# A mixture-of-experts kernel on one Trainium2 core: expert weights loaded tile by tile at a register's address, and held stationary in the up projections

## What is computed

```python
logits = xf @ gate_w.T                      # 8 experts
wts, idx = jax.lax.top_k(logits, 1)         # softmax over one: weight 1
h = silu(xf @ w1[e].T) * (xf @ w3[e].T)     # 128 -> 512, e the token's expert
y = h @ w2[e].T                             # 512 -> 128
y = y + gelu(xf @ sw1.T) @ sw2.T            # shared expert
```

## Time and profile before

| | us |
|---|---|
| median of three runs | 335.92 (335.11 to 340.64) |
| span of the profiled execution | 334.8 |
| PE busy | 234.4 (70%) |
| DVE busy | 170.4 (51%) |
| ACT busy | 106.4 (32%) |
| POOL busy | 102.7 (31%) |
| PE stage of the experts (first `turn_x` to the last `down`) | 252.2 to 326.9 |

### The profile page before, as it was taken

One profiled execution on the slowest core, in us unless ns is written; L12 is line 12 of the kernel. 1 busy time (PEld: TensorE's weight loads), 2 busy tenths in 40 slices (PEclk: granted clock), 3 DMA queues, 4 the chain that ended last, 5 costly groups with the idle time before them and its releaser, 6 DMA issues. The chain is left out here.

```text
span 334.8 us, 4486 instructions
## 1 busy us (share of the span) xinstructions
PE 234.4 (70%) x1436; PEld 125.6 (38%) x1436; DVE 170.4 (51%) x461; ACT 106.4 (32%) x215; POOL 102.7 (31%) x107
## 2 busy tenths in 40 slices
PE   0071673266197945979746989798946999999990
PEld 0050232112054412434213424356632665665650
DVE  7858999778036601467643772866011233423320
ACT  1000343000055441645432587342500223233230
POOL 9600178500047000640000000000751256556551
PEclk9996587555558585879785999979985899999997
DMA  6400059316163561636230079200222021121100
GB/s 200 148 0 1 0 145 166 130 53 143 72 144 108 141 161 57 133 91 158 71 88 10 5 243 405 109 2 0 81 79 77 25 58 37 43 53 35 35 15 0
DMA packets 21933, 29.46 MB, mean 88 GB/s; under 512 B 3306, under 2 KB 17200, under 8 KB 21912
## 3 DMA queue, kind: packets, MB, share of 16 engines
q1 hardware_dynamic: 20312, 26.81, 28.6%
q0 software_dynamic: 1600, 2.38, 2.7%
HBM read 21.14 MB, written 8.80 MB: 89 GB/s over the span
## 5 line engine op out<-in xcount | busy, mean ns | idle before, releaser
L669 DVE TENSOR_REDUCE smax<-bank 128x2 f32<-128x384 f32 x96 | 50.6, 554 | 59.1 <-PE bank L890 56.9
L476 ACT ACTIVATE p_ring<-bank 128x384 f32<-128x384 f32 x96 | 45.5, 491 | 73.5 <-PE bank L916 72.3
L890 PE MATMUL bank<-stacks 96*128 96x192 bf16 (+1 forms) x256 | 41.8, 316 | 35.2 <-DMA stacks<-split_scratch 33.0
L1067 PE MATMUL bank<-stacks,p_ring 128*128 x76 | 44.0, 666 | 2.1 <-DVE p_ring L792 1.8
L385 POOL TENSOR_TENSOR r<-f_ring,parts 128x384 f32<-128x384 f32 x14 | 12.8, 917 | 91.4 <-ACT f_ring L461 90.9
L890 PEld LDWEIGHTS bank<-stacks 96*128 96x128 bf16 (+1 forms) x256 | 16.5, 120 | 64.7 <-DMA stacks<-split_scratch 35.8
L410 POOL DMA_INDIRECT xs_scratch<-hn,slot_u x12 | 11.8, 982 | 90.4 <-issue 90.4
L916 PE MATMUL bank<-stacks 99*128 99x192 bf16 (+1 forms) x256 | 35.9, 277 | 2.7 <-ACT p_ring L476 2.4
L799 DVE TENSOR_TENSOR stacks<-bank,stacks 128x512 f32<-128x512 f32 x19 | 13.1, 691 | 45.5 <-PE bank L1067 45.5
L540 ACT ACTIVATE stacks<-bank 128x512 f32<-128x512 f32 x19 | 11.3, 597 | 61.8 <-PE bank L1067 61.8
L934 PE MATMUL bank<-p_ring,vaug 128*32 128x384 f32 (+1 forms) x256 | 29.5, 551 | 0.3 <-ACT oT L483 0.3
(11 more groups left out here) (127 smaller groups left out, 301.3 us busy)
## 6 DMA issues: line engine op xcount, KB each, us to landing
split_scratch<-parts SPq DMA_DIRECT2D x16, 288.0 KB, 9.8
stacks<-split_scratch SPq DMA_DIRECT2D x16, 288.0 KB
stacks<-in_w_dram SPq DMA_DIRECT2D x8, 512.0 KB, 7.9
stacks<-split_scratch SPq DMA_DIRECT2D x16, 192.0 KB
stacks<-in_w_dram SPq DMA_DIRECT2D x8, 256.0 KB, 8.1
stacks<-split_scratch SPq DMA_DIRECT2D x16, 96.0 KB
xs_scratch<-empty SPq DMA_DIRECT2D x19, 64.5 KB, 3.2
p_ring<-xs_scratch SPq DMA_DIRECT2D x19, 64.5 KB
```

What stands on the lines that cost most here:

```text
L476: act.activation(p_ring[:, half % 2, g % GH, :, :], bank[2 + g % 2][:, 0:2 * SEQ].rearrange("p (s q) -> p s q", s=2), ACT.Exp).then_inc(ex ...
L669: dve.tensor_reduce(smax[:, p % 2, j, 2 * hd:2 * hd + 2], bank[g % 2][:, 0:2 * SEQ].rearrange("p (s k) -> p s k", s=2), AX.X, ALU.max, neg ...
L890: ins = pe.matmul(bank[g % 2][r0:r0 + rn, SEQ * s:SEQ * (s + 1)], q_st[p % NST][0:SROWS, 2 * hd + s, 128 * j + r0:128 * j + r0 + rn], k_st ...
L1067: pe.matmul(bank[UP_BANKS[m][t % 2]][:, :], xsT[:, t % 2, :], w13_sb[:, bass.ds(e, 1), m, :].rearrange("p a i -> p (a i)"), start=True, st ...
```

## The change

Two things change, both in the expert stage.

1. The eight-expert load ahead of the stage is gone. `load_expert(t)` on SyncE reads `et_i[0, t]` into a register and loads that expert's `w13` and `w2` from DRAM into buffer t mod 3 (NW = 3). The first three are issued as soon as `et_i` is ready; from t = 3 on, `load_expert(t)` waits until `down(t-3)` is done (`y_mm`), and stands in SyncE's stream right behind `load_xs(t)`. All 19 tiles load their weights, also where neighbours have the same expert.
2. The up projections hold the weights stationary and move the 128 tokens: four matmuls of 128 columns in place of one of 512, for w1 and for w3. The result comes out with the 512 on the partitions, as `down` wants it, so `turn_g`, `copy_gT`, their PSUM bank and `gate_sb` are gone, and `gate` writes `gT` itself. PE's order becomes `up(t, 0)`, `turn_x(t+2)`, `up(t, 1)`, `down(t-1)`; the transposed tokens get a third buffer, and `take_x(t+2)` stands ahead of `gate(t)` on VectorE.

```diff
-            for e in range(E):
-                sp.dma_start(w13_sb[:, e, :, :], w13[e, :, :, :]).then_inc(ld_exp, 16)
-                sp.dma_start(w2_sb[:, e, :, :], w2[e, :, :, :]).then_inc(ld_exp, 16)
+            def load_expert(t):
+                if t >= NW:
+                    sp.wait_ge(y_mm, t - NW + 1)
+                e = sp.value_load(et_i[0:1, t:t + 1], min_val=0, max_val=E - 1)
+                sp.dma_start(w13_sb[:, t % NW, :, :], w13[bass.ds(e, 1), :, :, :].rearrange("a p m i -> p (a m) i")).then_inc(w_ld[t % NW], 16)
+                sp.dma_start(w2_sb[:, t % NW, :, :], w2[bass.ds(e, 1), :, :, :].rearrange("a p c d -> p (a c) d")).then_inc(w_ld[t % NW], 16)
...
+            sp.wait_ge(et_done, 1)
+            for t in range(NW):
+                load_expert(t)
             for tc in range(2):
...
             for t in range(NX, SLOT_TILES):
                 load_xs(t)
+                load_expert(t)
...
-            def copy_gT(t):
-                act.wait_ge(g_tr, t + 1)
-                if t >= 2:
-                    act.wait_ge(y_mm, t - 1)
-                act.activation(gT[:, t % 2, :], bank[GT_BANK][:, :], ACT.Copy).then_inc(g_cp, 1)
...
                 if t >= 2:
-                    dve.wait_ge(g_tr, t - 1)
-                dve.tensor_tensor(gate_sb[:, t % 2, :], bank[UP_BANKS[1][t % 2]][:, :], sA[:, t % 2, :], ALU.mult).then_inc(gated, 1)
+                    dve.wait_ge(y_mm, t - 1)
+                dve.tensor_tensor(gT[:, t % 2, :], bank[UP_BANKS[1][t % 2]][:, :], sA[:, t % 2, :], ALU.mult).then_inc(gated, 1)
...
             take_x(0)
+            take_x(1)
             for t in range(SLOT_TILES):
+                if t + 2 < SLOT_TILES:
+                    take_x(t + 2)
                 gate(t)
-                if t + 1 < SLOT_TILES:
-                    take_x(t + 1)
...
-            def up(t, e, m):
+            def up(t, m):
                 pe.wait_ge(x_cp, t + 1)
+                if m == 0:
+                    pe.wait_ge(w_ld[t % NW], 16 * 2 * (t // NW + 1))
...
-                pe.matmul(bank[UP_BANKS[m][t % 2]][:, :], xsT[:, t % 2, :], w13_sb[:, bass.ds(e, 1), m, :].rearrange("p a i -> p (a i)"), start=True, stop=True)\
-                    .then_inc(up_b if m else up_a, 1)
-
-            def turn_g(t):
+                for c in range(IC):
+                    ins = pe.matmul(bank[UP_BANKS[m][t % 2]][:, 128 * c:128 * (c + 1)], w13_sb[:, t % NW, m, 128 * c:128 * (c + 1)],
+                                    xsT[:, t % NXT, :], start=True, stop=True)
+                ins.then_inc(up_b if m else up_a, 1)
...
             for t in range(SLOT_TILES):
-                up(t, e, 0)
-                if t >= 1:
-                    turn_g(t - 1)
-                up(t, e, 1)
-                nxt = expert_of(t + 1) if t + 1 < SLOT_TILES else None
-                if t + 1 < SLOT_TILES:
-                    turn_x(t + 1)
-                if t >= 1:
-                    down(t - 1, prev)
-                e, prev = nxt, e
-            turn_g(SLOT_TILES - 1)
-            down(SLOT_TILES - 1, prev)
+                up(t, 0)
+                if t + 2 < SLOT_TILES:
+                    turn_x(t + 2)
+                up(t, 1)
+                if t >= 1:
+                    down(t - 1)
+            down(SLOT_TILES - 1)
```

More of the change, by code:

```diff
@@ L182, in build_kernel @@
         xs = carve("exp", NX, XW)
-        xsT = carve("exp", 2, D)
+        NXT = 3
+        xsT = carve("exp", NXT, D)
         sA = carve("stack", 2, I)
-        gate_sb = carve("stack", 2, I)
         gT = carve("exp", 2, I)
@@ L194, in build_kernel @@
         ld_x, ld_wn, ld_rows, ld_wp, ld_c, ld_txt, ld_np = [sem(f"ld_{n}") for n in ("x", "wn", "rows", "wp", "c", "txt", "np")]
-        ld_exp = sem("ld_exp")
+        w_ld = [sem(f"w_ld{i}") for i in range(NW)]
         dve_step, pool_step = sem("dve_step"), sem("pool_step")
@@ L227, in build_kernel @@
         xs_ld = [sem(f"xs_ld{i}") for i in range(NX)]
-        x_tr, x_cp, up_a, up_b, silu_done, gated, g_tr, g_cp, y_mm, y_cp = [sem(n) for n in (
-            "x_tr", "x_cp", "up_a", "up_b", "silu_done", "gated", "g_tr", "g_cp", "y_mm", "y_cp")]
+        x_tr, x_cp, up_a, up_b, silu_done, gated, y_mm, y_cp = [sem(n) for n in (
+            "x_tr", "x_cp", "up_a", "up_b", "silu_done", "gated", "y_mm", "y_cp")]
         id_done, base_clear, base_st = sem("id_done"), sem("base_clear"), sem("base_st")
@@ L251, in build_kernel @@
         SH_BANKS, SY_BANKS = (2, 3, 6, 7), (5, 0, 5)
[L252 removed]
+        UP_BANKS, XT_BANK, Y_BANKS, RANK_BANK = ((2, 3), (6, 7)), 4, (5, 0), 4
         def mbank(item):
@@ L789, in take_x @@
                 dve.wait_ge(x_tr, t + 1)
-                if t >= 2:
-                    dve.wait_ge(up_b, t - 1)
-                dve.tensor_copy(xsT[:, t % 2, :], bank[XT_BANK][:, 0:D]).then_inc(x_cp, 1)
+                if t >= NXT:
+                    dve.wait_ge(up_b, t - NXT + 1)
+                dve.tensor_copy(xsT[:, t % NXT, :], bank[XT_BANK][:, 0:D]).then_inc(x_cp, 1)
             def gate(t):
@@ L1066, in up, with down @@
                     pe.wait_ge(gated, t - 1)
-                pe.matmul(bank[UP_BANKS[m][t % 2]][:, :], xsT[:, t % 2, :], w13_sb[:, bass.ds(e, 1), m, :].rearrange("p a i -> p (a i)"), start=True, stop=True)\
-                    .then_inc(up_b if m else up_a, 1)
-            def turn_g(t):
-                pe.wait_ge(gated, t + 1)
-                if t >= 1:
[L1073 to L1079, removed]
+                for c in range(IC):
+                    ins = pe.matmul(bank[UP_BANKS[m][t % 2]][:, 128 * c:128 * (c + 1)], w13_sb[:, t % NW, m, 128 * c:128 * (c + 1)],
+                                    xsT[:, t % NXT, :], start=True, stop=True)
+                ins.then_inc(up_b if m else up_a, 1)
+            def down(t):
+                pe.wait_ge(gated, t + 1)
                 if t >= 2:
@@ L1085, in down @@
                     ins = pe.matmul(bank[Y_BANKS[t % 2]][:, 0:D], gT[:, t % 2, 128 * c:128 * (c + 1)],
-                                    w2_sb[:, bass.ds(e, 1), c, :].rearrange("p a d -> p (a d)"), start=(c == 0), stop=(c == IC - 1))
+                                    w2_sb[:, t % NW, c, :], start=(c == 0), stop=(c == IC - 1))
                 ins.then_inc(y_mm, 1)
[L1089 to L1093, removed]
             pe.wait_ge(sh_act, 3 * IC)
             turn_x(0)
-            e, prev = expert_of(0), None
+            turn_x(1)
             for t in range(SLOT_TILES):
-                up(t, e, 0)
+                up(t, 0)
+                if t + 2 < SLOT_TILES:
+                    turn_x(t + 2)
+                up(t, 1)
                 if t >= 1:
-                    turn_g(t - 1)
-                up(t, e, 1)
-                nxt = expert_of(t + 1) if t + 1 < SLOT_TILES else None
-                if t + 1 < SLOT_TILES:
-                    turn_x(t + 1)
-                if t >= 1:
-                    down(t - 1, prev)
-                e, prev = nxt, e
-            turn_g(SLOT_TILES - 1)
-            down(SLOT_TILES - 1, prev)
+                    down(t - 1)
+            down(SLOT_TILES - 1)
 def layouts(inputs):
```

8 lines of the change are left out of this document (3 added, 5 removed).

## The result

The changed kernel takes 417.9 us in the median of four runs (416.61 to 420.71), the kernel before 335.51 (334.91 to 340.64 in four): 1.25 times as long, 95% interval 1.243 to 1.256. The profiled execution has a span of 416.7 us against 334.8. The forecast was 411, range 383 to 431. Some executions of every kernel here took a few per cent longer at a lower clock; the ratios in this document leave those out on both sides, the medians and ranges don't.

The account below looks back on a forecast made before the run. PE bound the expert stage at 3.56 us a tile. Start to 262.9, 15 x 8.55 us to 391.2, last iterations to 402.5, ending 7.9 to 410.4; forecast 411 us, range 383 to 431.

Parts of the forecast that it names:

- The loads taken away ahead of the stage: Eight-expert load issued from 193.44: removing it gains nothing, since no one waited for it; first three new loads hidden.
- The new form: Expert stage matmuls: 0.91 us an up projection, 2.85 us a tile undisturbed against 3.56, 13.5 us gained at most.
- The ring: Iterations 2 to 16: `down` releases SyncE, whose token load behind the weights holds up PE; 8.55 us each; chance 0.79.
- both halves: Token load behind SyncE's wait for `down`, and `turn_x` wanting those tokens one iteration earlier, together make the ring.
- The path without PE: Ring's signal, register load, weight loads, tokens behind them and landing to PE: 5.23 us an iteration.
- PE's part at a clock of 0.61: `turn_x`, second up projection and `down` in the ring: 1.93/0.61 = 3.16 us, plus 0.16 until the last result.
- all at 0.50: Slow end of the range, PE's clock at 0.50 throughout: ring 9.25 us, total 423 us.
- The sum's other terms: Before the ring, start to 262.9; after it, last iterations from 391.2 to 402.5, then 7.9 us of ending.
- The tokens passing the weights: Rival at SyncE's token load: it lands 1.83 us after issue, ring 6.9 us, total 386 us; chance 0.09.
- PE staying the bound: Rival in the expert stage: load latency covered, period 2.85 us, total 322 us; chance 0.04.
- Slower loads: Rival at the weight loads: slow issue, 17 us more, or half of 417 GB/s, 28 us more, 440; chance 0.08.

Follow-up runs that it names:

- 320 us version: Changed kernel with six weight buffers, three filled behind the first token loads, four base buffers and base gathered three tiles ahead: 320.1 us, 0.948 times the kernel before.
- second chip: Another chip, running the 320 us version (329.8 us) and the same version with the kernel before's form of the matmuls (334.8 us).
- without the weights: Changed kernel without register load and weight loads from tile 3 on, SyncE's wait for `down` kept: 341.2 us, 1.005 times the kernel before.

## Why the prediction was right

The mechanism, its place and its sign were as forecast; the time was 6.3 us over the sum in the profiled execution (416.7 against 410.4). Point by point:

- *The loads taken away ahead of the stage give nothing, the first three are hidden.* Right: `turn_x(0)` starts at 251.39, before at 252.16.
- *The new form takes 0.91 us an up projection and 2.85 a tile.* Right, at full clock: 0.89 and 2.79 in the 320 us version, whose PE stage (251.6 to 306.3) is 20 us shorter than that of the kernel before. I had put the gain at 13.5 at most; 19 x (3.56 - 2.79) = 14.6 is the pace, the rest a quicker start. On the second chip the two forms were only 5 us apart; why stays open.
- *The ring.* Right in both halves, shown by taking each away. 15 waits at `turn_x`, 16 of SyncE for `down`, none for the weights at the up projections.
- *The path without PE, 5.23 us.* In the iteration shown it is 5.42 (325.62 to 331.04), in the mean of the 15 it is 5.56. `down` to the issue of `w13` 0.73 for 0.62; from there to the landing of `w2` 0.52 + 3.9 = 4.4 for 4.2; the tokens 0.2 later, as said; but PE starts 0.04 after the landing, for the 0.25 that I had taken from the stage's first tile. In the mean this term was 0.33 us an iteration too short, 5 us in all. The register load took 0.27, the median end, though SyncE came out of a wait each time. The floor of about 600 ns that the Trainium skill gives ("DMA: Bandwidth & Descriptors", list of measured latencies) doesn't hold for this load: 19 of them take 0.27 in the median here, 0.30 on PE before.
- *PE's part at a clock of 0.61.* This term was mis-sized: 3.32 us for 3.91 in the iteration shown (0.48 + 1.71 + 1.72) and 3.71 in the mean of the 15, since in some `down` or the up projection runs at full clock in part. That is 0.39 us an iteration, 6 us in all; with the 0.33 of the path it makes the 0.72 by which the period is longer. (The nine digits that I averaged give 0.60 and not 0.61, 1 us in the sum.) The average clock of the stage was even higher than I took, 0.69 to 0.72. But an average over the stage is the wrong number: `turn_x`, the second up projection and `down` stand right behind an idle stretch of some 4 us (63.6 us in 15 waits) and run mostly at 1.2 GHz; when the clock rises, it is `up(t, 0)` that gets it (1.39 and 1.06 us in rows of the timeline), and that lies beside the wait. Keeping PE busy showed it: full clock on those pieces, 1.3 us less an iteration. That the mean period is the 9.25 us of my end "all at 0.50" is partly chance: PE's part was 0.3 us shorter than there and the path 0.3 longer.
- *The sum's other terms.* The ring began 3 us sooner than said (`down(0)` ends at 259.9, not 262.9, since the clock rose earlier) and the end behind it was 1.5 us shorter (17.7 for 19.2). With 15 x 0.72 = 10.8 for the period: 10.8 - 3.0 - 1.5 = 6.3. So the total is closer than its terms, which erred both ways.
- *The rivals.* The tokens passing the weights: no, 3.7 us in the queue against 1.85 alone. PE staying the bound: not with this order, but it is what the next version reached. Slower loads: no, 3.9 us from issue to landing.

## What to carry to other kernels

When a queue issues several streams in order, write down for each transfer what the instructions ahead of it wait for, not only its own wait: here a small load stood behind a large one that waited for the end of the iteration, and its consumer had been moved one iteration ahead, so each iteration paid the whole latency. Issue the urgent small load first, and give the large one enough buffers that its wait is always over. And price matmuls by the clock that they get and not by the stage's average: behind waits of 4 us they ran mostly at the half clock here, behind waits of 1.1 us (without the weights) at the full one.

## What the runs showed of the hardware

- A mean clock says little of the critical pieces: 0.69 to 0.72 over the stage, 0.50 in most of the pieces on the chain. 3.7 us of useless matmuls in each wait held it at 0.96 to 1.00 and made the kernel 20 us faster.
- A register load and its arithmetic on SyncE took 0.27 + 0.15 + 0.02 us, and a DMA from a register's address 0.34 and 0.33 us to issue (`w13`, `w2`), no longer than from a fixed one (0.33 and 0.43).
- A 64.5 KB load lands 1.85 us after its issue alone, and 3.69 behind 768 KB on the same queue.
- The version that streams the weights took 320.1 and 318.0 us on two chips, on the first at 341 to 375 GB/s, and 329.8 on another, at 259 to 312 GB/s. The cause is open.
